# A six-layer stage in eight rounds a layer instead of nine, with paired floors and powers

## The reference, cut to what matters

```python
def attn_layer(x, Wqkv, qs, ksc, Wo):
    q, k, v = jnp.split(x @ Wqkv, 3, -1)              # 128 -> 3 * 1024
    q, k, v = (sh(q), sh(k), sh(v))
    q = l2norm(q) * qs
    k = l2norm(k) * ksc
    q = q * cos * scale + rotate_half(q) * sin * scale
    k = k * cos * inv + rotate_half(k) * sin * inv
    return local_attention(q, k, v).transpose(0, 2, 1, 3).reshape(b, n, INNER) @ Wo

def ffn_layer(x, g, bln, W1, b1, W2, b2):
    xn = (x - mu) / jnp.sqrt(var + 1e-05) * g + bln
    a, gate = jnp.split(xn @ W1 + b1, 2, -1)          # 128 -> 2 * 341
    return a * jax.nn.gelu(gate, approximate=False) @ W2 + b2

for i in range(6):
    x = attn_layer(shift_tokens(x), ...) + x
    x = ffn_layer(shift_tokens(x), ...) + x
```

## Time and profile before

| | |
|---|---|
| median of 3 runs | 2322.89 us |
| the profiled execution | 2328.08 us, of which 2326.2 us span |
| stage D in it | from 1222.8 us (first `DXS` copy on ACT) to the end |
| busy in the whole span | PE 1867.0 us, DVE 1716.5, ACT 1279.5, POOL 906.5 |
| L1279, add on POOL | 192 times, mean 1278 ns |
| L1281, power on POOL | 192 times, mean 1848 ns |
| L1567, first product on DVE | 192 times, mean 764 ns |

### The profile page before, as it was taken

One profiled execution on the slowest core, in us unless ns is written; L12 is line 12 of the kernel. 1 busy time (PEld: TensorE's weight loads), 2 busy tenths in 40 slices (PEclk: granted clock), 3 DMA queues, 4 the chain that ended last, 5 costly groups with the idle time before them and its releaser, 6 DMA issues. The chain is left out here.

```text
span 2326.2 us, 52273 instructions
## 1 busy us (share of the span) xinstructions
PE 1867.0 (80%) x18512; PEld 924.7 (40%) x18512; DVE 1716.5 (74%) x3041; ACT 1279.5 (55%) x1850; POOL 906.5 (39%) x913
## 2 busy tenths in 40 slices
PE   5745888888888888888846887887888888788786
PEld 3531222222222222222223654654655555555564
DVE  4744677767777777777648988878878887887893
ACT  4411665656666666666635655645546555555553
POOL 0012111111111111111028858648657666675670
PEclk9955898989999999999958998999999999999998
DMA  1002223232222232222004323323323333232330
GB/s 34 1 24 61 46 56 61 56 59 55 59 55 59 55 59 55 59 55 57 2 30 119 92 85 92 87 85 92 94 87 92 86 93 92 68 111 75 84 84 10
DMA packets 88745, 152.83 MB, mean 66 GB/s; under 512 B 16819, under 2 KB 51669, under 8 KB 84693
## 3 DMA queue, kind: packets, MB, share of 16 engines
q1 hardware_dynamic: 86421, 149.04, 26.2%
q10 hardware_dynamic: 2112, 0.94, 0.2%
HBM read 98.03 MB, written 51.12 MB: 64 GB/s over the span
## 5 line engine op out<-in xcount | busy, mean ns | idle before, releaser
L899 DVE TENSOR_REDUCE ENM<-PM 128x1 f32<-128x512 f32 x1024 | 658.4, 685 | 257.2 <-PE PM L722 248.8
L819 ACT ACTIVATE EPT<-PA 128x1024 f32<-128x1024 f32 x512 | 512.4, 1021 | 220.2 <-PE PA L734 137.6
L722 PE MATMUL PM<-EKX,EQX 48*128 48x512 bf16 x1024 | 356.3, 402 | 104.3 <-DVE ENM L899 84.0
L1279 POOL TENSOR_TENSOR DQR<-DR 128x512 f32<-128x512 f32 x192 | 245.4, 1278 | 289.0 <-DVE DR L1569 289.0
L1281 POOL TENSOR_TENSOR DRN<-DRN,DHALF 128x8 f32<-128x8 f32 x192 | 354.8, 1848 | 8.4
L642 POOL CAST ENMP<-ENM 128x16 bf16<-128x16 f32 x64 | 12.6, 196 | 786.2 <-DVE ENM L899 786.2
L744 PE MATMUL PV<-EPT,EVP 128*32 128x512 f32 x2048 | 286.7, 633 | 0.8 <-ACT EPT L819 0.7
L734 PE MATMUL PA<-EQX,EKX 51*128 51x512 bf16 x1024 | 254.8, 397 | 28.4 <-DMA EQX<-EROWS 15.9
L722 PEld LDWEIGHTS PM<-EKX,EQX 48*128 48x128 bf16 x1024 | 85.8, 95 | 482.1 <-DVE ENM L899 392.7
L1325 PE MATMUL PM<-DWQKV,DXS 128*128 128x512 f32 x384 | 218.0, 651 | 47.3 <-ACT XNT L1526 29.2
L1487 ACT ACTIVATE DRAW<-PM 128x512 f32<-128x512 f32 x192 | 114.7, 598 | 143.4 <-PE PM L1325 106.4
(11 more groups left out here) (208 smaller groups left out, 2960.9 us busy)
## 6 DMA issues: line engine op xcount, KB each, us to landing
DV<-d_vpark SPq DMA_DIRECT2D x192, 256.0 KB, 5.0
d_vpark<-DVT SPq DMA_DIRECT2D x48, 512.0 KB, 2.6
e_park<-EPARTS SPq DMA_DIRECT2D x64, 192.0 KB, 2.9
EQX<-e_park SPq DMA_DIRECT2D x32, 384.0 KB, 5.5
EKX<-e_park SPq DMA_DIRECT2D x32, 384.0 KB, 9.2
DWQKV<-in_WqkvR SPq DMA_DIRECT2D x6, 1536.0 KB, 9.5
e_park<-EPARTS SPq DMA_DIRECT2D x64, 128.0 KB, 2.7
e_park<-EPARTS SPq DMA_DIRECT2D x64, 64.0 KB, 2.1
```

What stands on the lines that cost most here:

```text
L722: pe.matmul(PM[:, r, :], lhsT=QX[64 * r:64 * r + KQ, b, hp, t * 128:(t + 1) * 128], rhs=KX[64 * r:64 * r + KQ, b, hp, :], start=True, stop ...
L819: s_.activation(PT[:, kt, pair * 2 * S:(pair + 1) * 2 * S], PA[:, 2 * pair:2 * pair + 2, :].rearrange("p a b -> p (a b)"), ACT.Exp, scale= ...
L899: v.tensor_reduce(NM[:, g % 2, t, j, 0:1], PM[:, r, :], AX.X, ALU.max, negate=True).then_inc(maxed, 1)
L1279: g.tensor_tensor(qr, r1, r2, ALU.add).then_inc(roped.sem if queries else joined.sem, 1)
```

## The change

1. **Eight rounds a layer.** PERIOD becomes 8. Round 8 of a layer, which had no new projection, falls together with round 0 of the next: in it the turns of the old tile 7 and the chunks of the new tile 0 alternate.
2. **A new order within a round.** Mix comes behind c0 instead of c1, the output product and the output add ahead of c3 instead of behind it. The normalisation is split (`f1b` statistics behind the score block, `f1c` behind the mix), and `f1b` to `f4` of a batch entry stand in one round; DVE's part of `f3` is a piece of its own (`f3v`), behind c3.
3. **Piecewise reloads and tables.** The weights are loaded in six pieces of 512 columns, each once the last tile's chunk has been multiplied; the table of a batch tile t is formed on POOL in rounds 5, 6, 7 and 0, when the last use of the old one is over. The first layer's scales are loaded ahead of its weights.
4. **The second product in one instruction** of 512 columns, with the halves read in reverse order.
5. **Floor and power for two chunks at once**: 16 columns, behind c1 and behind c3. For keys both scalings follow the common power.

```diff
-PERIOD = NT + 1
+PERIOD = NT
...
+    for c in range(4):
+        for k in range(NT + 1):
+            order.append((k, 10 * (c + 1), "proj", (k, c)))
+        order.append((NT - 1, 10 * (c + 1) + 4, "weights", c))
+    for n in range(NT):
+        order += [(n, 48, "vout", n), (n + 1, 5, "vin", n)]
+        order += [(n + 2, 0, "score", n), (n + 2, 21, "exp", n), (n + 2, 33, "weigh", n)]
+        order += [(n + 3, 9, "pturn", n), (n + 3, 14, "mix", n), (n + 3, 24, "oturn", n), (n + 3, 35, "out", n)]
+    for b in range(B):
+        k = TB * b + TB + 2
+        order += [(TB * b, 1, "shift", b), (k, 45, "f1a", b), (k + 1, 6, "f1b", b), (k + 1, 16, "f1c", b), (k + 1, 26, "f2", b)]
+        for c, (at, then) in enumerate(((36, 41), (42, 43), (44, 45))):
+            order += [(k + 1, at, "f3", 3 * b + c), (k + 1, then, "f3v", 3 * b + c)]
+        order.append((k + 1, 49, "f4", b))
...
@@ POOL, a chunk
                         queries = n[1] < 2
                         g.tensor_tensor(qr, r1, r2, ALU.add).then_inc(roped.sem if queries else joined.sem, 1)
-                        pool.wait_ge(floored.sem, floored.at(layer, k))
-                        g.tensor_tensor(rn, rn, HALF[:, 0:8], ALU.pow).then_inc(rooted.sem, 1)
-                        if not queries:
-                            pool.wait_ge(joined.sem, joined.at(layer, 2 * n[0] + n[1] - 2))
-                            pool.wait_ge(rooted.sem, rooted.at(layer, k))
-                            g.tensor_tensor(qr.rearrange("p (h e) -> p h e", h=8), qr.rearrange("p (h e) -> p h e", h=8),
-                                            bc(rn, 2, [128, 8, DL]), ALU.mult).then_inc(roped.sem, 1)
+                        if n[1] % 2:
+                            rn = RN[:, n[0] % 2, 8 * n[1] - 8:8 * n[1] + 8]
+                            pool.wait_ge(floored.sem, floored.at(layer, k // 2))
+                            g.tensor_tensor(rn, rn, HALF[:, :], ALU.pow).then_inc(rooted.sem, 1)
+                        if n[1] == 3:
+                            for c in range(2):
+                                qr = QR[:, (k - 1 + c) % 4, :].rearrange("p (h e) -> p h e", h=8)
+                                pool.wait_ge(joined.sem, joined.at(layer, 2 * n[0] + c))
+                                pool.wait_ge(rooted.sem, rooted.at(layer, k // 2))
+                                g.tensor_tensor(qr, qr, bc(rn[:, 8 * c:8 * c + 8], 2, [128, 8, DL]), ALU.mult).then_inc(roped.sem, 1)
...
@@ DVE, a chunk
-                        v.tensor_tensor(r2[:, :, 0:32], x[:, :, 32:64], bc(tab[:, 1, 0:32], 1, [128, 8, 32]), ALU.mult).then_inc(step, 1)
-                        v.tensor_tensor(r2[:, :, 32:64], x[:, :, 0:32], bc(tab[:, 1, 32:64], 1, [128, 8, 32]), ALU.mult).then_inc(rotated.sem, 1)
+                        v.tensor_tensor(halves(r2), halves(x)[:, :, ::-1, :], bc(tab[:, 1].rearrange("p (s e) -> p s e", s=2), 1, [128, 8, 2, 32]),
+                                        ALU.mult).then_inc(rotated.sem, 1)
                         wait(squared, k)
-                        v.tensor_reduce(SS[:, k % 2, :], SQ[:, k % 2, :].rearrange("p (h e) -> p h e", h=8), AX.X, ALU.add).then_inc(summed.sem, 1)
-                        wait(summed, k)
-                        v.tensor_scalar(RN[:, n[0] % 2, 8 * c:8 * c + 8], SS[:, k % 2, :], 1e-24, None, ALU.max).then_inc(floored.sem, 1)
+                        v.tensor_reduce(SS[:, k // 2 % 2, 8 * (c % 2):8 * (c % 2) + 8], SQ[:, k % 2, :].rearrange("p (h e) -> p h e", h=8), AX.X, ALU.add).then_inc(summed.sem, 1)
+                        if c % 2:
+                            wait(summed, k)
+                            v.tensor_scalar(RN[:, n[0] % 2, 8 * c - 8:8 * c + 8], SS[:, k // 2 % 2, :], 1e-24, None, ALU.max).then_inc(floored.sem, 1)
```

More of the change, by code:

```diff
@@ L1079 @@
+    for t in range(TB):
+        order.append((TB + 1 + t, 2, "table", t))
+    order += [(1, 30, "scales", None), (NT + 2, 49, "output", None), (NT + 4, -1, "late", None)]
+    return sorted(order, key=lambda x: x[:2])
 FIRST = [(0, name, n) for k, at, name, n in layer_order() if k < PERIOD]
@@ L1232, in piece @@
                         late(nxt)
-                early(slice(0, 1))
+                scales(slice(0, 1))
+                for c in range(4):
+                    weights(slice(0, 1), c)
                 output(slice(0, 1))
@@ L1732 @@
     qs, ks = a["L1_ffn_q_scale"], a["L1_ffn_k_scale"]
[L1733 removed]
+    d["scales"] = again(np.stack([qs, swap(qs), ks, swap(ks)], 1))
     c = np.zeros((DEPTH, 128, 8), np.float32)
```

108 lines of the change are left out of this document (42 added, 66 removed).

## The result

The changed kernel takes 2393.26 us (median of 4 runs, 2385.71 to 2396.19) against 2326.23 of the kernel before (median of 4). The ratio is 1.0281, 95% interval 1.0242 to 1.0320. The direction was forecast, the size was not: 2339 was predicted, with 2374 as the upper end.

The account below looks back on a forecast made before the run. DVE was taken to bound the even rounds (16.63 of 17.20 us). Terms +0.6 - 4 x 0.1 + 3.2 + 12.3 = +15.7 on the profiled 2328.1 gave 2343.8, less 5.2 for the median: 2339 us; 8-in-10 range 2285 to 2374.

Parts of the forecast that it names:

- The power of 2.94 us: On POOL, a power of 16 columns: 0.16 us a column and 0.35 fixed, so 2.94 us.
- Both floors blocked: On DVE, the floors behind c1 and c3 are both held by POOL's add: 1.34 us a round instead of 1.5.
- Both scalings back to back: On POOL, c2 and c3 are scaled after the subtract, ahead of the next c0: 0.7 us more an even round.
- the add of c2 behind the power: On POOL, c2's add waits for the power of c0 and c1, holding c3's first product: 1.4 us more an even round.
- The even round of 18.8 us: A round without feed-forward work takes 18.8 us instead of 17.2.
- the layer of 181.3 us: A middle layer: eight rounds of 18.8 us plus feed-forward, loop-end and table terms, 181.3 us against 181.5 before.
- a rival of 0.10: PE falls to 1.2 GHz more often, one stretch a layer and half more, 4 us each: 2375 us, chance 0.10.
- One f3 chunk follows another by 2.0 us: Feed-forward block behind c3: chunk spacing of 0.75 + 1.27 us, with f4 ending at 9.1 us.
- The gelu's delay of c3: In the feed-forward round, c3's copy must wait for the gelu, so c3 starts 1.8 us later.
- The last layer: At the kernel's end: +3.2 us to the first batch entry's f4, then +12.3 us for round 8.
- the faster one: Even rounds fall better, near PE's 17.8 us, if the 16-column power is below about 2.3 us: 2293 us, chance 0.27.
- The third: POOL's power keeps DVE out throughout, some +2.2 us in 46 rounds: 2440 us, chance 0.03.

Follow-up runs that it names:

- the filled kernel: The changed kernel with eight unread products on PE ahead of its wait for the weighted mix: 2350.15 us, ratio 1.0093 to the kernel before.
- both cured: The changed kernel with the gate/value chunks of `f3` spread and eight unread products on PE ahead of the mix wait: 2313.30 us, ratio 0.9931.

## Why the prediction was too low

Its own steps, one by one.

**What held.** The second product's direction (11 us alone by the ratio, 3 by stage D; 13 reckoned). The power of 2.94 us (2.91). Both floors blocked (mean 760 ns of 96). Powers don't keep DVE out. Both scalings back to back with c0 behind them, and the add of c2 behind the power: shown apart as +0.7 and +1.7 in even rounds of nine (0.7 and 1.4 reckoned), though the +0.7 is a mean of three unlike rounds and near the term in part by luck. The even round of 18.8 us: two of a layer take 18.73 at full clock once PE is kept busy, another 18.20. Reloads and tables next to nothing. The first layer came out shorter than reckoned (158.05 against 161.4).

**The step that failed: the layer of 181.3 us.** It was 190.05. The overlap was wrong in two ways: the even rounds gave no price to PE's standing still, neither in the clock behind it nor in the copies that then come late, and the feed-forward block had its chunks 2.0 us apart. An experiment undid each by itself.

- *PE's standing still.* The forecast took every round at 2.4 GHz and put PE's lower clock into a rival of 0.10, because "the TensorE rows of the even rounds speak against it". They were rows of before. The forecast itself said that PE would stand still 2 us more in each round. It stood still for 2.32 us ahead of the weighted mix (1.23 in the same round of before) and went on at 1.2 GHz. The trace of before had such a stretch already, with a product pair of 1.91 us instead of 1.02 behind a wait, though in the first round of a layer and not in an even one:

```profile
1769.99 0.33 PE L144 MATMUL PA<-IDENT,DP 128*128 128x128 f32 x1 [2.46 <-DVE DP L1595]
...
1771.45 1.91 PE L1325 MATMUL PM<-DWQKV,DXS 128*128 128x512 f32 x2
```

  That rival's size (36 us) is near what the filled kernel gives back (44 us by the ratio, 27 in stage D). Part of this nearness is luck. The time at 1.2 GHz in all of stage D barely grew (134 to 140 us), and the filled kernel also loses the pauses, which the forecast did not have at all. So the wait was named and given nothing in the sum; how its price divides between clock and pauses stays open.
- *The feed-forward block.* "One f3 chunk follows another by 2.0 us", and f4 was to end 9.1 us behind c3's second product. In the middle of a layer it ended 11.5 behind (1845.11 to 1856.6), and c0's second product of the next tile began 17.9 behind instead of 15.3 (1845.11 to 1863.04). At the loop end that was 24.4 instead of 22.3 (1940.21 to 1964.60). The spacing of 2.0 came from a stretch of before in which PE had not stood still. In the new order its value product waits for a DVE piece behind c3's sum and floor, and the three products behind that wait ran at the lower clock (two at the loop end). The gelu's delay of c3 was 1.8 in the forecast; the wait was 3.29 and 1.94. Spreading the chunks gave back 39 us (27.5 in stage D).

By the ratios the two give back 83 us together, by stage D of the traces 60.4 (1157.5 to 1097.1). Stage D was forecast at 1119.1, so 38.4 were to be explained, and the rest of the forecast was too high: with both cured a layer is 178.2 us, not 181.3, and the first one 153.95. Where these 3.1 us a layer were over-reckoned was not settled; the rounds of 18.20 and the cured feed-forward round of 29.30 are the likeliest places.

**The last layer** was +22.4 us, 15.5 forecast. The end part was well sized: from the last f4 of batch entry 0 to tile 7's score block it took 15.5 us instead of 1.8, +13.7 (12.3 forecast). The rest is the longer layer ahead of it, +9.3 instead of +3.2.

**The rivals.** Of the condition for the faster one (a power below 2.3 us) nothing came. The third, that the power keeps DVE out, did not happen. The second is above.

**What stays open.** In nine rounds the pairs cost 65 us and the early mix 64, whatever the clock; together with eight rounds and the compressed feed-forward block they do not add up to more than 65. The runs show where each bites, but not why, in eight rounds and once the two losses are gone, the early mix is 23 us better than the late one by the ratios and the pairing makes no difference. What makes PE pause is open. The eight rounds themselves were never run alone, without the new order.

## What to carry to other kernels

When a part of a change makes an in-order engine stand still longer, price what it does afterwards at the clock that it has after such a wait, and look for PE rows behind a wait of that length in the same trace. In a pipeline whose three main engines are 84 to 97% busy in a round, a new order is judged by which wait stands ahead of work that someone else needs next: a wait that is placed one chunk earlier cost 64 us with no instruction added. And run the parts apart: of the parts that were, one brought 11 us, one nothing, and two cost 64 and 65, and the sum read +65. Last, when a single cure works, look at what else it changed: here both the clock and the pauses.
